# Local attention of a hybrid transformer block: a new order of each engine's steps within a tile

## What is computed

```python
def attn_layer(x, Wqkv, qs, ksc, Wo):          # 16 heads of 64, window 32
    q, k, v = split(x @ Wqkv)
    q = l2norm(q) * qs;  k = l2norm(k) * ksc
    q = q * cos * scale + rotate_half(q) * sin * scale
    k = k * cos / scale + rotate_half(k) * sin / scale
    out = local_attention(q, k, v)             # each window of 32 looks at itself and the one before
    return out @ Wo
for i in range(DEPTH):
    x = attn_layer(shift_tokens(x), ...) + x
    x = ffn_layer(shift_tokens(x), ...) + x
```

## Time and profile before

| | |
|---|---|
| time, median of 3 runs | 7207.77 us (7205.19 to 7207.87) |
| the profiled execution | 7208.77 us |
| its span on the core | 7206.7 us |
| local attention | 12 layers of 16 tiles, the first exps at 918.45, the last at 6167.6 us |
| TensorE matmul busy | 5312.7 us (74%) |
| ScalarE, VectorE busy | 3985.0 us (55%), 3840.9 us (53%) |
| GpSimd busy | 2396.7 us (33%) |

### The profile page before, as it was taken

How to read it: one execution, slowest core, us unless ns; L and a number is a source line. 1 busy time by engine, 2 the same in 40 slices (tenths; PEclk the granted TensorE clock), 3 DMA queues, 4 the chain that set the end, 5 groups by cost and what they waited for, 6 DMA issues and landing times. The chain is left out here.

```text
span 7206.7 us, 178920 instructions
## 1 busy us (share of the span) xinstructions
PE 5312.7 (74%) x69288; PEld 3368.6 (47%) x69288; DVE 3840.9 (53%) x6202; ACT 3985.0 (55%) x8451; POOL 2396.7 (33%) x1351
## 2 busy tenths in 40 slices
PE   1000198888888888977777988888888979687778
PEld 0000065655656564733333655656564747343444
DVE  5555654645455554555554645455554546445854
ACT  4333264646455555539997646555554546355655
POOL 0000162626354444504443626354453535000000
PEclk6555599999999999976666989999998989766876
DMA  1000121212222121200000212212121212000000
GB/s 43 0 0 0 37 51 48 55 49 54 53 49 59 42 53 50 57 11 1 1 1 20 55 47 53 54 45 52 47 57 44 57 45 57 18 2 3 0 2 6
DMA packets 177838, 248.52 MB, mean 34 GB/s; under 512 B 51692, under 2 KB 79848, under 8 KB 175080
## 3 DMA queue, kind: packets, MB, share of 16 engines
q1 hardware_dynamic: 177128, 237.68, 13.2%
HBM read 43.50 MB, written 5.24 MB: 7 GB/s over the span
## 5 line engine op out<-in xcount | busy, mean ns | idle before, releaser
L377 PE MATMUL PS<-arena 128*128 128x512 f32 x2304 | 1163.5, 632 | 220.0 <-ACT arena L500 117.1
L670 POOL TENSOR_TENSOR arena<-arena 128x512 f32<-128x512 f32 x384 | 586.6, 1551 | 651.3 <-DVE arena L622 651.3
L670 POOL TENSOR_TENSOR lns<-arena 128x512 f32<-128x512 f32 x384 | 566.1, 1498 | 666.7 <-DVE arena L622 666.7
L377 PEld LDWEIGHTS PS<-arena 128*128 128x128 f32 x2304 | 412.9, 199 | 646.1 <-issue 359.7
L499 ACT ACTIVATE arena<-PS 128x512 f32<-128x512 f32 x768 | 472.1, 615 | 333.4 <-PE PS L377 258.4
L434 PE MATMUL PS<-arena 64*64 64x32 f32 x24576 | 534.7, 227 | 155.4 <-ACT arena L531 121.4
L592 DVE TENSOR_REDUCE arena<-PS 128x16 f32<-128x1024 f32 x192 | 235.2, 1225 | 731.0 <-PE PS L408 731.0
L1106 PE MATMUL PS<-arena 128*128 128x512 f32 x8 | 6.7, 1019 | 807.8 <-DVE arena L1040 807.8
L434 PEld LDWEIGHTS PS<-arena 64*64 64x64 f32 x24576 | 509.5, 141 | 191.7 <-issue 188.0
L611 DVE TENSOR_REDUCE arena<-arena 128x32 f32<-128x2048 f32 x192 | 438.8, 2285 | 293.4 <-ACT arena L500 286.1
L539 ACT ACTIVATE arena<-PS 128x512 f32<-128x512 f32 x384 | 208.9, 597 | 648.0 <-PE PS L434 648.0
(11 more groups left out here) (254 smaller groups left out, 11101.2 us busy)
## 6 DMA issues: line engine op xcount, KB each, us to landing
arena<-arena SPq DMA_DIRECT2D x2880, 64.0 KB, 2.0
arena<-in_L_ffn_Wqkv SPq DMA_DIRECT2D x12, 1536.0 KB, 6.5
arena<-in_L_ffn_Wo SPq DMA_DIRECT2D x48, 128.0 KB, 6.3
scratch<-arena SPq DMA_DIRECT2D x4, 1024.0 KB, 4.8
arena<-scratch SPq DMA_DIRECT2D x4, 1024.0 KB, 7.6
arena<-in_L_ffn_W SPq DMA_DIRECT2D x12, 341.0 KB
arena<-in_ffn_scales SPq DMA_DIRECT2D x12, 128.0 KB, 5.8
arena<-in_L_ffn_W SPq DMA_DIRECT2D x12, 128.0 KB
```

What stands on the lines that cost most here:

```text
L377: pe.matmul(PS[:, QKV + n % 2, :], xs[uu % 2][:, par * P:(par + 1) * P], w, start=True, stop=True).then_inc(qkv_ready, 1)
L670: last = pool.tensor_tensor(heads(t2)[:, :, a:a + 32], heads(raws[par])[:, :, b:b + 32], sine, ALU.mult)
```

## The change

The same instructions run in a new order. TensorE takes projection chunks one at a time between turned blocks, has both groups of scores ahead of the heads, and the last projection chunk at the end of the tile. ScalarE starts the tile with `exps`, follows TensorE's new order, copies the probabilities ahead of chunk 4 and of `rnorm`, does `enter` before the copies of the heads, and ends with chunk 5. VectorE does `softmax_shift` ahead of `unit_length`. The code before the loop is unchanged.

```diff
--- before.py
+++ after.py
@@ -451,21 +451,29 @@
                 for tt in range(TILES):
                     ahead = not (final and tt + 1 >= TILES)
                     further = not (final and tt + 3 >= TILES)
-                    for half in range(2):
-                        if further:
-                            qkv(g, tt + 3, (2 * half, 2 * half + 1))
-                        if ahead:
-                            turn_qk(g, tt + 1, (2 * half, 2 * half + 1))
                     if further:
-                        qkv(g, tt + 3, (4, 5))
+                        qkv(g, tt + 3, (0,))
+                    if ahead:
+                        turn_qk(g, tt + 1, (0, 1))
+                    if further:
+                        qkv(g, tt + 3, (1, 2))
+                    if ahead:
+                        turn_qk(g, tt + 1, (2,))
+                    if further:
+                        qkv(g, tt + 3, (3,))
+                    if ahead:
+                        turn_qk(g, tt + 1, (3,))
+                    if further:
+                        qkv(g, tt + 3, (4,))
                     turn_probs(g, tt, final)
                     if ahead:
                         scores(g, tt + 1, 0)
+                        scores(g, tt + 1, 1)
                     heads(g, tt, final)
-                    if ahead:
-                        scores(g, tt + 1, 1)
                     if tt % 2 == 1:
                         project(g, tt // 2)
+                    if further:
+                        qkv(g, tt + 3, (5,))
             wait_alone(pe, attn_w_loaded, (run + 1) * ATTN_LOADS)
             for tt in range(3):
                 qkv(run * BODIES, tt, range(6))
@@ -550,25 +558,33 @@
                 for tt in range(TILES):
                     ahead = not (final and tt + 1 >= TILES)
                     further = not (final and tt + 3 >= TILES)
+                    exps(g, tt)
                     if further:
-                        copy_qkv(g, tt + 3, (0, 1), True)
-                    exps(g, tt)
+                        copy_qkv(g, tt + 3, (0,), True)
                     if ahead:
-                        copy_turned(g, tt + 1, (0, 1))
+                        copy_turned(g, tt + 1, (0,))
                     if further:
-                        copy_qkv(g, tt + 3, (2, 3), True)
+                        copy_qkv(g, tt + 3, (1,), True)
+                    if ahead:
+                        copy_turned(g, tt + 1, (1,))
+                    if further:
+                        copy_qkv(g, tt + 3, (2,), True)
                     if ahead:
                         copy_turned(g, tt + 1, (2, 3))
                     if further:
-                        copy_qkv(g, tt + 3, (4, 5), True)
+                        copy_qkv(g, tt + 3, (3,), True)
+                    copy_probs(g, tt, final)
+                    if further:
+                        copy_qkv(g, tt + 3, (4,), True)
                         rnorm(g, tt + 3)
-                    copy_probs(g, tt, final)
+                    if tt % 2 == 0 and not (final and tt + 4 >= TILES):
+                        enter(it * UNITS_IN_BODY + (tt + 4) // 2, (tt + 4) // 2 % 2)
                     copy_heads(g, tt, 0)
                     copy_heads(g, tt, 1)
                     if tt % 2 == 1:
                         copy_projected(g, tt // 2)
-                    elif not (final and tt + 4 >= TILES):
-                        enter(it * UNITS_IN_BODY + (tt + 4) // 2, (tt + 4) // 2 % 2)
+                    if further:
+                        copy_qkv(g, tt + 3, (5,), True)
             first = run * BODIES
             enter(0, 0)
             enter(1, 1)
@@ -628,12 +644,15 @@
 
             def body(g, it, final):
                 for tt in range(TILES):
+                    ahead = not (final and tt + 1 >= TILES)
+                    further = not (final and tt + 3 >= TILES)
                     softmax_norm(g, tt, nth(g, TURN_PER, place_probs(tt - 1, 1, False)))
-                    if not (final and tt + 3 >= TILES):
+                    if further:
                         norms(g, tt + 3)
+                    if ahead:
+                        softmax_shift(g, tt + 1)
+                    if further:
                         unit_length(g, tt + 3)
-                    if not (final and tt + 1 >= TILES):
-                        softmax_shift(g, tt + 1)
                     if tt % 2 == 1:
                         add_stream(g, it, tt // 2)
             wait_alone(dve, tables_ready, run + 1)
```

## The result

The changed kernel takes 7237.83 us (median of 6 runs, 7225.77 to 7261.44); the kernel before, on the same chip, takes 7206.48 us. The ratio is 1.0046, with a 95% interval of 1.0025 to 1.0066, so the change makes the kernel slower by about half a per cent, where I had forecast half a per cent faster. A second set of runs on another chip gave 1.0044 (1.0027 to 1.0061). The profiled execution took 7261.44 us, 23.6 us above the median and 52.7 us above the profiled one of before (7208.77 us). I compare the two profiles, so their difference is some 21 us larger than that of the medians (31 us). The profiled execution is also the one with the lowest mean clock of its six (0.816; the other five have 0.820 to 0.824), so it shows more half clock than an average execution of this kernel.

The account below looks back on a forecast made before the run. TensorE was taken to set the pace in the steady part. Steady pairs -8, first tiles -5 and last tiles -23 summed to -36 us, giving 7172 us (-0.5%), range 7115 to 7235 us.

Parts of the forecast that it names:

- Step 1: Dense run: the heads' wait for copied probabilities goes, part returns as "issue"; even tiles 0.52 us less.
- rival (d): Dense runs without a pause meet two refill stops; in a third of steady runs +74, 7246 us; chance 0.16.
- Step 2: Odd tiles: the projection waits 0.7 us for ScalarE's copy of the heads; 0.41 us more a tile.
- Steps 3 and 5: Chunks alternating with turned blocks, enter early, chunk 5 last: copies hide by 0.6 us or more, nothing lost.
- Step 4: VectorE's shift first: L606 meets GpSimd's rotate, but EN stays hidden with 1.2 us to spare.
- Step 6: First tile of a layer: wait before heads goes, chunk 2 waits about 1.2 us; net -0.4 a layer, -5 us.
- Step 7: Last tiles of a layer: tile 13 -1.1, its projection +0.7, tile 15 -1.5; -23 us, clock left as is.
- (b): Instruction refill entirely hidden, so dense runs cost the bare sum: -1.7 us a pair, 7059 us; chance 0.02.
- (e): ScalarE's or VectorE's cover too short by 0.5 us a tile: some +72, 7244 us; chance 0.07.

Follow-up runs that it names:

- e4: Changed kernel with chunk 5 between the heads and the projection, ScalarE's order likewise: 7192.12 us, ratio 0.9957 to before.
- e9: Changed kernel with chunk 4 between first scores and heads, then chunk 5 and the second scores behind the heads: 7267.73 us, ratio 1.0059 to before.
- e8: Changed kernel with VectorE's old order (unit_length ahead of softmax_shift) everywhere: 7239.76 us, ratio 1.0010 to before.
- e16: Changed kernel with VectorE's old order in the last body alone: 7218.60 us, ratio 1.0006 to before.
- e11: Kernel before, with a last body that has TensorE's and ScalarE's new order and VectorE's old one: 7175.58 us, ratio 0.9940 to before.
- e2: Kernel before in the loop bodies, the whole new order in the last body: 7201.04 us, ratio 0.9970 to before.
- e1: New order in the three loop bodies, the order of before in the last body: 7266.63 us, ratio 1.0067 to before.
- e5: Changed kernel with TensorE's hardware loop written out, so no branch is left in it: 7281.06 us, ratio 1.0066 to before.
- e6: Kernel before with one edit, ScalarE copies the probabilities ahead of chunks 4, 5 and rnorm: 7215.62 us, ratio 0.9971 to before.
- e3: Changed kernel with ScalarE's copy of the probabilities back behind chunk 4 and rnorm: 7723.63 us, ratio 1.0690 to before.

## Why the prediction was wrong, step by step

- **Step 1, the wait goes: right. What comes back as "issue": too low.** L539, now the copy of the probabilities, ends 11.6 us, none of it in the steady part. Even runs of tiles 2, 6 and 10 take 5.9 to 6.2 us on average, close to the predicted 5.95. But tiles 4 and 8 take 7.15 to 7.5. I had one such run in the trace of before, 7.5 us in the earlier trace rows, and gave it to rival (d) with a chance of 0.16, as one that decides from 23 of 144 runs. It occurs in tiles 4 and 8 of every layer, 24 runs, that is just at rival (d)'s point of balance: 24 x (7.35 - 5.95) = 34 us. The step's mistake was to take the length of a run from tiles 13 and 14, whose place in the code is another. **This is the step that failed:** "Even tiles: 6.47 - 5.95 = 0.52 us less". Over the 60 even runs of tiles 2 to 10 the difference is +0.04 us a run, +0.10 in the second profile: +2 and +6 us where the step had -31. Only four of these runs have any half clock in them in the first profile, and two in the second.
- **Step 2, the projection pays: right.** 65.4 us over 96 projections, 0.68 us each. Odd runs with it are 6.4 to 6.8 us; predicted 6.58. Against before the odd runs lengthen by 0.29 us, where step 2 had 0.41, as they took 6.37 us on average before and not the 6.17 of the pair shown: +21 us in the steady part, predicted +30. e4 took 49 us of this idle away and gained 64 (46 to 82).
- **Steps 3 and 5: right.** L377's idle is 218.8 us (220.0 before), and none of it is behind a copy in the steady part. e9 shows the cover from the other side.
- **Step 4: right in the steady part.** The product EN takes 2.02 us there instead of 1.34, yet the transposes stand for it in none of the tiles 0 to 11, and e8, with the old order everywhere, is no faster than e16, which has it in the last body alone.
- **Step 6** can't be seen by itself: the first tiles' dense run has no wait for L539 now, but stops of 0.5 to 1.9 us instead; it is 7.53 us long on average, before 7.86, so -4 us in sum.
- **Step 7, the tail: the wait ahead of tile 15 was right (5.00 us; predicted about 5), that ahead of tile 13 had the wrong sign, and the clock was left out.** I had tile 13's idle shrink by 1.1 us, since the scores end earlier. EN's product begins 1.0 us before TensorE wants it, now (1155.12 against 1156.12) as before (1153.62 against 1154.61): nothing was gained there, and it is held by GpSimd 1.2 us longer: 2.45 instead of 1.23 us. The idle is 1.8 to 2.5 us in all twelve layers, and behind it the clock fell to half: tile 13, from its transposes to those of tile 14, took 20.6 to 22.1 us in seven layers of this profile, 18.9 in one and 15.5 to 15.8 in four; before it took 14.9 to 15.7. e16 and e11 show that this is VectorE's order, and that without it the tail is worth -28 (e11) to -41 us (e16), more than the predicted -23. Summed over the layers, the idle ahead of tile 13 rose by 19 us (predicted -13), that ahead of tile 15 fell by 19 (predicted -18). That e2 still shows the last body near the predicted -23 is luck, in part at least: the idle ahead of the turned blocks (L392), all of it in the tail, fell from 33.5 to 10.9 us, which no step of mine had.
- **The sum.** Two terms failed. The larger is step 1's gain in the even tiles: -37 us over 72 pairs, of which nothing came. e1 has the same loop and shows the loss by itself: +48 us for the loop, against -13. The other is in step 7 with "I leave the clock as it is": tile 13's wait grew by 1.2 us instead of shrinking by 1.1, and the half clock followed it, which I had put at nothing. e16 sizes the two together, with VectorE's order as the cause: 0.40% or 28 us, within some 17 us. In the first profile the clock looks like the largest term (up to 71 us, where the stages together grew by 56), but that was the execution with the lowest clock; over all executions on the second chip it explains some 5 us of the loss and at most 18.
- **The rivals.** (b) is refuted by e5 and e6. (d) is right in mechanism and in its count of runs: it takes away the gain of the steady part (+8 us apart from the clock in the first profile and +19 in the second, where I had -13). (e) didn't happen in the steady part of the changed kernel, but its form (VectorE's product held by GpSimd) is what happened in tile 13. The loss as a whole has no rival of mine: it is (d) in the loop, the projection's wait that step 2 had, and in the last body a longer wait with the half clock behind it.

What stays open: why the stretch between layers takes 20 us longer in both profiles, for which no step had a term (TensorE's idle time there is 8 and 11 us more; at half clock it has 297 and 294 us, before 242, e16 with the same loop 263, and there is only one profile of before). Nor does any run change the clock alone, so its share of the loss in the loop and in the last body is worked out and not shown.

## What to carry to other kernels

Price idle time of TensorE with the clock that it may cost: in this kernel 169 us more of it, in waits of 1.75 us a tile, came with 309 us more busy time for the same matmuls (e3 against the changed kernel). Compare clocks over several executions, though: one profile made the clock look like the main cause here, and ten did not. Where many small matmuls follow each other, put a few large ones between them, if the copies that those feed stay covered; chunk 5 between scores and heads, with the copy of the probabilities ahead, brought 1.1% where this change lost 0.5%. And cost a removed wait by the engine's next limit at *each* place in the code, not by one sample run.

## What the runs showed of the hardware

**TensorE stops by itself in long rows of small matmuls.** In the changed kernel a stop is 0.2 to 1.7 us long, and the stops lie at the same few matmuls of a tile in layer after layer; in tiles 4 and 8 there are mostly two or three of them, some 126 matmuls apart. They end 2.2 to 2.9 us after a 16 KB packet of the instruction queue has begun, 2.4 in the middle. A packet began 2.1 to 2.6 us earlier for 72% of the stops, and for 6% of moments picked at random. That is a coincidence in time far beyond chance, and no proof of a cause. Totals of "issue" ahead of L434 and L408: 62 us before, 119 changed, 141 in e6, 142 without a loop, 20 with two chunks spread into the run. The Trainium skill, page "Runtime: NRT & Kernel Launch", section "Instruction fetch mechanics", calls the cost of crossing a 16 KiB boundary mostly hidden and a taken branch a reason for a stall; here the runs don't agree with the first, and by e5 the branch isn't what makes these stops.

**The half clock follows small idle times, not only long ones.** Take the idle time of TensorE in the first 11 us of a steady tile, rounded to half a microsecond, in all profiles but e3's. A stretch at 0.5 began in none of the 315 tiles with next to none, in 45 of the 830 with about 1 us, and in 28 of the 66 with about 2 us or more; no sharp limit shows. Before this case I had expected them behind idle times such as the 6.57 us of the earlier trace rows alone.

**VectorE's product of two SBUF operands waits for GpSimd's current instruction.** It ends 1.1 us behind it in all 85 cases before and all 168 in the changed kernel in which it begins beside one: 2.09 us before and 3.32 us now in tile 13, 1.23 us alone. The Trainium skill, page "GPSIMD Engine Reference", section "8. Key points", names this contention; how much it costs is in the rows.
